# Layer 0 takes x of batches 1 to 7 channel-major from DRAM, with its row statistics turned by a small scratch

## What is computed

```python
# layer 0 (layer 1 differs in the attention)
xn = layernorm(x) * ln_w + ln_b
q = softmax(xn @ Wq + bq, over the 64 channels of a head)
k = softmax(xn @ Wk + bk + mask, over the tokens)
v = (xn @ Wv + bv) * mask
y = q @ (k^T @ v)                       # per head
scale, shift = split(silu(emb) @ W_emb + b_emb)
h = layernorm(y) * (1 + scale) + shift  # ln2_w, ln2_b inside
x = x + silu(h) @ W_out + b_out
```

## Time and profile before

| | before |
|---|---|
| median of 3 runs | 1351.97 us (1345.44 to 1352.27) |
| profiled execution | 1352.28 us, span 1350.5 us |
| TensorE busy | 1311.5 us (97%) |
| VectorE busy | 950.1 us (70%) |
| ScalarE busy | 966.7 us (72%) |
| GpSimd busy | 345.2 us (26%) |
| mean granted clock | 0.967 of full speed |
| chain that ended last | TensorE 75%, ScalarE 12%, VectorE 6%, GpSimd 3%, DMA 1% |

### The profile page before, as it was taken

The page is one execution under the profiler, slowest core; times in us unless marked ns, Lnnn a source line. Parts: engine busy times, 40 slices in busy tenths (PEclk is TensorE's granted clock), DMA queues, the critical chain, the costliest instruction groups (busy, mean ns, idle before and its releaser), DMA issues.

```text
span 1350.5 us, 25321 instructions
## 1 busy us (share of the span) xinstructions
PE 1311.5 (97%) x9592; PEld 1048.4 (78%) x9592; DVE 950.1 (70%) x1930; ACT 966.7 (72%) x2147; POOL 345.2 (26%) x367
## 2 busy tenths in 40 slices
PE   8999999999999999899999999999999999999998
PEld 5788888888888876577787787787787787786666
DVE  5756766666676766666876876876876876877556
ACT  5444344354434548788998998999999999998884
POOL 0323234432334460100500501501501501400302
PEclk9999999999999999899999899899899899899879
DMA  9111111211112356755455455555555545554512
GB/s 336 49 40 63 40 63 62 80 63 40 63 40 87 110 180 190 218 173 158 152 163 158 153 162 158 163 152 158 165 150 158 175 141 157 170 145 126 161 37 87
DMA packets 83994, 173.76 MB, mean 129 GB/s; under 512 B 7304, under 2 KB 8328, under 8 KB 83872
## 3 DMA queue, kind: packets, MB, share of 16 engines
q1 hardware_dynamic: 83872, 172.14, 41.1%
HBM read 104.45 MB, written 67.14 MB: 127 GB/s over the span
## 4 chain that ended last, share of the span: by engine, by line
PE 75%; ACT 12%; DVE 6%; POOL 3%; issue 2%; DMA 1%; SPq 0%; DVEq 0%; POOLq 0%; ACTq 0%
PE ps L526 15%; PE ps L528 14%; PE ps L527 14%; PE ps L705 9%; ACT ps L872 7%; PE ps L521 6%; PE ps L679 6%; PE ps L687 6%; ACT Pb L882 3%; PE ps L630 2%; PE ps L612 2%; POOL yb L1293 1%; DVE st L984 1%; DVE cT L1120 1%; PE ps L540 1%
## 5 line engine op out<-in xcount | busy, mean ns | idle before, releaser
L872 ACT ACTIVATE ps<-ps,cT 128x512 f32<-128x512 f32 x512 | 352.4, 769 | 22.9 <-DVE cT L1120 22.9
L1120 DVE TENSOR_REDUCE cT<-ps 128x1 f32<-128x512 f32 x512 | 321.6, 682 | 66.1 <-PE ps L679 65.8
L882 ACT ACTIVATE Pb<-ps 128x512 f32<-128x512 f32 x512 | 271.3, 669 | 38.4 <-PE ps L687 37.8
L679 PE MATMUL ps<-Ks,Qs 98*128 98x512 f32 x512 | 198.6, 449 | 18.2 <-ACT ps L872 14.7
L679 PEld LDWEIGHTS ps<-Ks,Qs 98*128 98x128 f32 x512 | 100.2, 198 | 80.2 <-ACT ps L872 49.1
L687 PE MATMUL ps<-Qs,Ks 100*128 100x512 f32 x512 | 158.9, 407 | 2.9 <-DVE sg_q L1111 1.2
L872 ACT ACTIVATION_READ_ACCUMULATOR ps<-ps,cT 128x1 f32 x512 | 161.5, 315 | 0.0
L1293 POOL TENSOR_TENSOR yb<-yb,cU 128x512 f32<-128x512 f32 x14 | 20.6, 1486 | 428.0 <-DVE cU L1166 428.0
L687 PEld LDWEIGHTS ps<-Qs,Ks 100*128 100x128 f32 x512 | 95.6, 189 | 38.2 <-ACT Pb L882 11.3
L526 PE MATMUL ps<-xTh,Wh_k 128*128 128x512 f32 x256 | 108.6, 424 | 5.5 <-DVE Wl_k L922 2.9
L1217 POOL TENSOR_TENSOR rs<-ve,mhalf 128x4 f32<-128x4 f32 x32 | 33.0, 1031 | 286.3 <-DVE ve L969 222.8
(11 more groups left out here) (159 smaller groups left out, 2718.0 us busy)
## 6 DMA issues: line engine op xcount, KB each, us to landing
Qs<-stack_scratch SPq DMA_DIRECT2D x32, 768.0 KB
Ks<-stack_scratch SPq DMA_DIRECT2D x32, 768.0 KB
stack_scratch<-sg_q SPq DMA_DIRECT2D x32, 512.0 KB, 2.7
stack_scratch<-sg_k SPq DMA_DIRECT2D x32, 512.0 KB, 2.6
wr<-in_x SPq DMA_DIRECT2D x32, 256.0 KB, 5.0
x_scratch<-wr SPq DMA_DIRECT2D x32, 256.0 KB, 2.0
stack_scratch<-sg_q SPq DMA_DIRECT2D x32, 256.0 KB, 2.9
stack_scratch<-sg_k SPq DMA_DIRECT2D x32, 256.0 KB, 2.9
```

Source lines behind the costliest of these rows:

```text
L679: e.matmul(bank[:], Qs[par][0:RX, j, t * 128:(t + 1) * 128], Ks[par][0:RX, j, :], start=True, stop=True).then_inc(s["S"], 1)
L872: e.activation(bank[:], bank[:], ACT.Exp, bias=nx[:, n % 2, j, t, 0:1], accum_out=dn[:, b % 2, t, 4 * g + j:4 * g + j + 1]).then_inc(s["S_ ...
L882: e.activation(Pb[m][:, j, :], ps[bank_of["a", n, m, j]][:], ACT.Exp).then_inc(s["P"], 1)
L1120: e.tensor_reduce(nx[:, n % 2, j, t, 0:1], ps[bank_of["S", n, j, t]][:], AX.X, ALU.max, negate=True).then_inc(s["S_max"], 1)
```

## The change

For x of batches 1 to 7 (`turned_on_host`) a second DRAM input `xT0` holds x channel-major. Its tile `xr` (1 MB) is loaded beside the token-major `xin`, which is now read by bn_stats only. The two columns per token tile (1/sqrt and -mean/sqrt) are written by GpSimd into `lnc`, turned by four 32 x 32 transposes of VectorE, stored by SP to a DRAM scratch of 2 x 512 values and read back as rows on all 128 partitions (`rn`). A new part `xn`, in the q stage, multiplies and adds these rows on GpSimd, two full-tile operations for each of 4 tiles. Part `tx` has no TensorE work for these batches: VectorE scales and shifts `xr` with ln_w and ln_b, ScalarE copies it to `xTh`, and VectorE writes `xTl` as the difference of two SBUF tiles. The load of the next x waits for the statistics and, with that of the next `xr`, stands behind the last `xTl`. The positions of layer 0's stages and of the seam are other numbers.

```diff
-    "0k": ((0.063, 0.764), (0.503, 1.092)),
-    "0v": ((0.889, 1.145), (0.111, 0.562)),
-    "0q": ((0.659, 1.176), (0, 0.263), (1.065, 1.134)),
-    "0o": ((1.083, 1.166), (0.409, 1.001), (0.43, 0.514)),
+    "0n": ((0.297, 0.652),),
+    "0k": ((0.107, 0.69), (0.373, 0.41)),
+    "0v": ((0.566, 0.962), (0.081, 0.694)),
+    "0q": ((0.486, 0.575), (0.077, 0.696), (1.149, 1.191)),
+    "0o": ((0.67, 0.724), (0, 0.57), (0.041, 0.346)),
...
               ([("mb", 0, 1)] if first else [], 0.1, 0.75),
+              ([] if last else [("xn", b + 1)], *PLAN["0n"][0]),
...
+def turned_on_host(x):
+    return 0 < x < 8
...
+    if k == "tx" and turned_on_host(p[1]):
+        return [], []
...  TensorE
             def tx(i, x, c):
-                if i == 0:
+                if i == 0 and not turned_on_host(x):
...  ScalarE, tx
+                    if turned_on_host(x):
+                        e.wait_ge(s["x_f"], 4 * (x - 1) + c + 1)
+                        e.copy(xTh[:, c, :], xr[:, c, :]).then_inc(s["xT_hi"], 1)
+                        return
...  VectorE, nx
+                if i == 5 and turned_on_host(x):
+                    e.wait_ge(s["x_nr"], x + 1)
+                    if x > 1:
+                        e.wait_ge(s["l_ln0"], 16 * (x - 1))
+                    for u in range(4):
+                        r = e.transpose(lnT[:, 32 * u:32 * u + 32], lnc[32 * u:32 * u + 32, :])
+                    r.then_inc(s["x_T"], 1)
...  VectorE, tx
+                if i == 0 and turned_on_host(x):
+                    p = cols[0]
+                    e.wait_ge(s["xn"], 4 * x + c + 1)
+                    e.tensor_scalar(xr[:, c, :], xr[:, c, :], p[:, c:c + 1], p[:, 4 + c:5 + c],
+                                    ALU.mult, ALU.add).then_inc(s["x_f"], 1)
+                if i == 1 and turned_on_host(x):
+                    e.wait_ge(s["xT_hi"], 4 * x + c + 1)
+                    e.tensor_tensor(xTl[:, c, :], xr[:, c, :], xTh[:, c, :].bitcast(F32), ALU.subtract).then_inc(s["xT_lo"], 1)
+                    return
...  GpSimd
+                    e.tensor_tensor(lnc[:, 0:4], ve[:, 0, :], mhalf[:], ALU.pow).then_inc(s["x_rs"], 1)
...
+                    e.tensor_tensor(lnc[:, 4:8], nm[:, 0, :], lnc[:, 0:4], ALU.mult).then_inc(s["x_nr"], 1)
...
+            def xn(i, x):
+                if i == 0:
+                    e.wait_ge(s["l_ln1"], 16 * x)
+                    e.wait_ge(s["l_xT"], 16 * x)
+                e.tensor_tensor(xr[:, i, :], xr[:, i, :], rn[:, 0, :], ALU.mult).then_inc(s["x_m"], 1)
+                e.wait_ge(s["x_m"], 4 * (x - 1) + i + 1)
+                e.tensor_tensor(xr[:, i, :], xr[:, i, :], rn[:, 1, :], ALU.add).then_inc(s["xn"], 1)
...  SP, tx
-                    e.wait_ge(s["tx"], 4 * x + 4)
+                    if x == 0:
+                        e.wait_ge(s["tx"], 4)
+                    else:
+                        e.wait_ge(s["x_st"], 4 * x + 4)
+                        e.wait_ge(s["xT_lo"], 4 * x + 4)
                     load_x(x + 1)
+                    e.dma_start(xr[:], A["xT0"][x + 1]).then_inc(s["l_xT"], 16)
+
+            def nx_(i, x):
+                if i == 6 and turned_on_host(x):
+                    e.wait_ge(s["x_T"], x)
+                    e.dma_start(lnd.rearrange("a (t n) -> (a t) n", t=NT), lnT[0:8, :]).then_inc(s["l_ln0"], 16)
+                    e.wait_ge(s["l_ln0"], 16 * x)
+                    if x > 1:
+                        e.wait_ge(s["xn"], 4 * x)
+                    e.dma_start(rn[:], lnd.partition_broadcast(128)).then_inc(s["l_ln1"], 16)
```

More of the change, by code:

```diff
@@ L297, in cond_two_layers @@
         qkd = nc.dram_tensor("stack_scratch", [2, 2, 4, RM, T], F32, kind="Internal").ap()
+        lnd = nc.dram_tensor("ln_scratch", [2, T], F32, kind="Internal").ap()
         x1d = nc.dram_tensor("x1_scratch", [B, T, D], F32, kind="Internal").ap()
@@ L355, in cond_two_layers @@
         mB = sb("mB0", [128, T], c=c0)
-        sb("over_sg", [128, NC, D], c=c0)
+        xr = sb("xr", [128, NC, T], c=c0)
         sp = [sb(f"sp{i}", [128, D], c=c0) for i in range(3)]
@@ L369, in cond_two_layers @@
         qrc = sb("qrc", [128, 2, H0], c=c0)
+        rn = sb("rn", [128, 2, T], c=c0)
+        lnc = sb("lnc", [128, 32], c=c0)
+        lnT = sb("lnT", [32, 128], c=c0)
         c0.close()
@@ L406, in l_x, with tx_count @@
             return (s["l_x1"], n) if x % 2 else (s["l_x0"], 16 * 7 + n)
+        def tx_count(x, c):
+            return c + 1 if x == 0 else 4 * (x - 7) + c + 1
         def e_mod(L, h):
@@ L794, in v @@
                         if t == 0:
-                            e.wait_ge(s["tx"], 4 * x + 4)
+                            e.wait_ge(s["tx"], tx_count(x, 3))
                         if x == 8 and t == 0:
@@ L895, in prologue @@
                 e.memset(A0[:], 0.0).then_inc(s["a_set"], 1)
+                e.memset(lnc[:], 0.0).then_inc(s["ln_set"], 1)
                 e.memset(nxs[:].bitcast(F32), 0.0).then_inc(s["nx_set"], 1)
@@ L965, in nx_ @@
                 if i == 4:
-                    if x:
+                    if x == 1 or x > 8:
                         e.wait_ge(s["xn"], 4 * x)
+                    elif x:
+                        e.wait_ge(s["x_nr"], x)
                     e.wait_ge(s["x_mv"], 4 * x + 4)
@@ L1222, in nx_ @@
             def nx_(i, x):
+                if i == 4 and turned_on_host(x):
+                    e.wait_ge(s["x_ve"], x + 1)
+                    if x > 1:
+                        e.wait_ge(s["x_T"], x - 1)
+                    else:
+                        e.wait_ge(s["ln_set"], 1)
+                    e.tensor_tensor(lnc[:, 0:4], ve[:, 0, :], mhalf[:], ALU.pow).then_inc(s["x_rs"], 1)
+                    e.wait_ge(s["x_nm"], x + 1)
+                    e.wait_ge(s["x_rs"], x + 1)
+                    e.tensor_tensor(lnc[:, 4:8], nm[:, 0, :], lnc[:, 0:4], ALU.mult).then_inc(s["x_nr"], 1)
+                    return
                 if i == 4:
                     scales("x", 0, x)
-                if i > 4 and x:
+                if i > 4 and x >= 8:
                     t = i - 5
@@ L1296, in _ @@
             prologue()
-            parts = {"nx": nx_, "ny": ny, "q": q, "qn": qn, "o": o, "ty": ty, "ones": ones, "tlx": tlx}
+            parts = {"nx": nx_, "xn": xn, "ny": ny, "q": q, "qn": qn, "o": o, "ty": ty, "ones": ones, "tlx": tlx}
             for p, i in order:
@@ L1381, in tx @@
                 if i == 1 and c == 3 and x < 7:
-                    e.wait_ge(s["tx"], 4 * x + 4)
-                    load_x(x + 1)
+                    if x == 0:
+                        e.wait_ge(s["tx"], 4)
+                    else:
+                        e.wait_ge(s["x_st"], 4 * x + 4)
+                        e.wait_ge(s["xT_lo"], 4 * x + 4)
+                    load_x(x + 1)
+                    e.dma_start(xr[:], A["xT0"][x + 1]).then_inc(s["l_xT"], 16)
[4 more added lines that the diff above has]
+                    e.wait_ge(s["l_ln0"], 16 * x)
+                    if x > 1:
+                        e.wait_ge(s["xn"], 4 * x)
+                    e.dma_start(rn[:], lnd.partition_broadcast(128)).then_inc(s["l_ln1"], 16)
             def k(i, b, g):
@@ L1414, in ahead @@
                     e.wait_ge(s[f"st{t}"], 16)
-                e.wait_ge(s["tx"], 32)
+                e.wait_ge(s["x_st"], 32)
                 load_x(8)
@@ L1483, in _ @@
             prologue()
-            parts = {"w": w, "m": m, "tx": tx, "k": k, "ty": ty, "o": o, "ahead": ahead, "stacks": stacks, "narrow": narrow, "qk": qk,
+            parts = {"w": w, "m": m, "nx": nx_, "tx": tx, "k": k, "ty": ty, "o": o, "ahead": ahead, "stacks": stacks, "narrow": narrow, "qk": qk,
                      "stack": stack, "nxt": nxt, "lx": lx, "lr": lr, "end": end}
@@ L1514 @@
         "cols1": np.concatenate([col(g[P1 + n]) for n in ("norm_w", "norm_b", "sb_norm_w", "sb_norm_b", "q_b", "k_b", "emb_b")], axis=1),
+        "xT0": np.ascontiguousarray(g["x"].transpose(0, 2, 1).reshape(B, NC, 128, T).transpose(0, 2, 1, 3)),
         "Wq0": g[P0 + "Wq"], "bq0": g[P0 + "bq"], "Wk0": g[P0 + "Wk"],
```

6 lines of the change are left out of this document (3 added, 3 removed), and 4 rows, old and new, of tables (COST, PLAN).

## The result

| | before | after |
|---|---|---|
| median of the runs | 1351.97 us | 1362.61 us (1358.99 to 1363.81) |
| ratio of the medians | | 1.0083 [1.0061, 1.0105] |
| profiled execution | 1352.28, span 1350.5 | 1362.31, span 1360.5 |

The prediction was 1372 in a range of 1345 to 1386, with 0.66 on slower. The side came out, and so did what holds TensorE up; the size is 10.0 us between the two profiled spans, where the sum said 19.8.

A forecast was written before the change was run, and what follows sets the result against it. TensorE's queue was taken to bound layer 0. Middle batches +11.1, batch 0 to 1 +10.0, seam +0.2 and -1.5 make +19.8 us on 1352.28: 1372; own range 1360 to 1384, 1345 to 1386 including the covered case.

The forecast's parts named there:

- undisturbed the chain fits by about 1 us: Middle batches: without turns, last xTl ready at 28.2 us after q's first product, k wanting its fourth at 29.6.
- the scratch and the burst of statistics: Middle batches, k stage: statistics burst and DRAM round trip cost nothing; the burst's ends 0 and 1 us a batch.
- the value of the transposes: Middle batches: TensorE's 16 transposes of x go, 1.75 us a batch, 10.5 us over batches 2 to 7.
- the clock in the middle batches: Layer 0's middle batches: the forecast's sum has no term for a lowered TensorE clock there.
- The stall: k's third and fourth steps wait for xTl, 3.6 us a batch (0 to 4.5), net +1.85 with the transposes gone.
- The replay: o stage with VectorE and GpSimd taking strict turns: subtractions end at 23.5, 26.2, 29.6, 33.1 us after q's first product.
- The third rival: Waits at k's third and fourth steps also lower the clock in each batch, 6 to 10 us more: 1380, chance 0.18.
- Batch 0 to 1: No o stage covers the chain there: k's fourth step +8.3 us, clock +1.7, together +10.0, ends 4 and 12.
- The lower end of 4: Batch 0 to 1: least loss, 4 us, if the statistics row is back from DRAM at once.
- The seam and layer 1: Seam to layer 1: new order -1.5 us (ends -4 and +3), two more changes between products and small blocks +0.2.
- The cover holds: Rival: turns cost the middle batches nothing, 6 x -1.75, batch 1 costs 5.9 plus 1.7 clock: 1348, chance 0.21.
- Faster: Rival: cover holds, scratch returns early and clock stays up, batch 1 costs about 2, seam gives 3: 1341, chance 0.13.

The follow-up runs named there:

- experiment 1: Kernel after, but ScalarE writes xTh and the full value into PSUM and VectorE only subtracts: 1342.16 us, 0.9943 of the kernel before.
- experiment 2: Kernel after without GpSimd's bias sums of o in layer 0 but for one column (result wrong): 1346.73 us, 0.9981 of the kernel before.
- experiment 5: Kernel after without turning and storing the statistics, other DRAM rows loaded instead (statistics wrong): 1359.39 us, 1.0070 of the kernel before.
- experiment 6: Kernel after, but batch 1 prepared the old way with TensorE's transposes: 1351.81 us, 1.0015 of the kernel before.
- experiment 4: Kernel after with GpSimd's second pass over x, the sum, cut to one column: 1348.76 us, 1.0003 of the kernel before.
- experiment 3: Kernel after, but ScalarE writes xTh and the full value back to xr in SBUF, VectorE only subtracts: 1342.50 us, 0.9951 of the kernel before.
- experiment 8: Kernel after with the full value in PSUM for batches 2 to 7 and batch 1 the old way: 1336.52 us, 0.9906 of the kernel before.
- experiment 7: Kernel before with only the changed kernel's positions in layer 0's stages and the seam: 1348.97 us, 0.9991 of the kernel before.

## Why the prediction was right, and where its sizes were off

**What was right.** The cause in the middle batches is the one replayed from the earlier trace rows: VectorE and GpSimd take turns when both work between SBUF tiles. Experiments 1 and 2 show it from both sides, by taking away VectorE's part and half of GpSimd's part of the pairing; experiment 2 alone, with VectorE's work untouched, gives 1.6 of the 2.24 us back. The Trainium skill's page "SBUF — State Buffer", section "SBUF: two separate sides", states the lock. The trace agrees: a subtraction lasts 0.64 us alone and 0.99 to 1.40 beside GpSimd in the timeline above, and in experiment 1 its mean with one operand in PSUM is 0.68. That undisturbed the chain fits by about 1 us was not run as such: experiment 1 fits, but has the scaling on ScalarE. GpSimd's first subtraction came 5.9 us after q's first product (5.8 forecast) and its fourth ended at 20.4 (20.5). That the scratch and the burst of statistics cost the middle batches nothing was right (experiment 5), and so was the value of the transposes: 1.80 us at equal positions and 1.68 against the kernel before, for a forecast of 1.75.

**Luck.** The forecast put the clock in the middle batches at nothing, and it gave 3.2 us of the 10.0. Without these the difference would be 6.8 us, a third of the forecast. On the other side the tail of the profiled execution came out 3.4 us short through the clock, as said below. The two happen to cancel.

**The stall: 2.24 us instead of 3.6.** The replay had k's third step 0.8 and its fourth a further 2.8 us late. The trace has 0 and 2.12 (138.18 against 135.28 + 0.78, the distance of undisturbed steps), with 0.1 for the restart. The step that failed is the length of the turns in the replay, one after another. After q's first product, the four subtractions end at:

| tile | replay | trace |
|---|---|---|
| 0 | 23.5 | 23.2 |
| 1 | 26.2 | 25.8 |
| 2 | 29.6 | 28.7 |
| 3 | 33.1 | 31.8 |

The replay charged VectorE most of a GpSimd instruction each time. In the timelines above GpSimd's is mostly well under way when VectorE asks: the third scaling starts at 132.06 beside a normalisation that runs since 131.67, and the second subtraction (131.50) finds GpSimd waiting for VectorE's reciprocal and lasts 0.64. That saves 0.3 us on the first tiles and 1.3 by the last. The replay also had k ask for its fourth tile at 29.6, where the trace has 29.75, which takes off the rest. The bounds, 0 to 4.5, held it. The net is +0.57 us a batch instead of +1.85.

**The clock in the middle batches: +3.2 us, which the forecast had at nothing.** The third rival said that a rest of some 2 us brings the clock down, each time. It does so in two of the six batches (and in two of six again in experiments 5 and 6, which have the same wait); in none of the six of experiment 4, whose waits are 1.1 to 1.5 us. There the period is 60.2 instead of 58.6, and behind the wait that ends at 196.75 the clock stands low:

```profile
196.00:200.00 4.00, 3.25 (x13) 2.77 (x14) 3.93 (x9) 0.95 (x2) 1.85 (x2) 0.73 0.32 108
200.00:204.00 4.00, 4.00 (x26) 3.67 (x25) 1.35 (x3) 1.50 (x3) 0.00 (x0) 0.84 1.06 396
```

(1 - 0.73) x 4 + (1 - 0.84) x 4 = 1.7 us, the 1.6 of the period. The four other batches rest for the same 1.95 us and keep 1.00. Without a wait (experiments 1, 3 and 8) no period is longer than 56.35. Why two and not six isn't settled. The middle batches thus lost 6 x 0.57 + 2 x 1.6 = 6.6 us: 3.4 by a smaller stall than forecast, less the transposes, and as much again through the clock.

**Batch 0 to 1: +8.3 instead of +10.0.** The links are those of the forecast, and the sizes are these. The power came at 47.48 (46.71 was assumed) and the store was issued at 49.74; it landed within 1.2 us, where 2.0 was taken from the earlier trace rows. GpSimd had the rows at 54.48, where 56.0 was forecast. The broadcast of 512 KB took 3.6 us, less than the 4.5 of the mask's 256 KB. Its source is 4 KB; whether that is why was not tried. From there it took 16.3 us to k's first step (16.5 forecast) and 6.95 to its fourth (7.3). The last tile took no turn, because GpSimd has no bias sums at this boundary: a scaling of 0.54 and a subtraction of 0.69 us. The clock cost 2.0 (1.7 forecast). The planner's numbers, which the prediction had at nothing here, gave 1.07 back (experiment 7). The lower end of 4, for a row that is back at once, was too low: in experiment 5 GpSimd doesn't wait for the row at all, and the loss is 5.2 (55.91 - 50.72).

**The seam and layer 1: -4.9 instead of -1.3.** By its share this is the term that was most off, and it lies outside its lower end of -4. It falls into three stretches:

| | before | after |
|---|---|---|
| q of batch 7 to q of layer 1 | 78.5 | 77.9 |
| from there to the first power of layer 1 | 118.05 | 114.4 |
| from there to the end | 707.8 | 707.1 |

Most of it is the granted clock of these two executions. Summed over windows from q of batch 7 to the end, TensorE stands at 1.2 GHz for 82 us before and for 75 in after. Half of such time is lost, if TensorE is wanted throughout: 41.0 and 37.6 us by this estimate, 3.4 of the 4.9 (1.7 of it in the second stretch). That much comes and goes without any change: in 25 runs of the kernel before the mean clock of the whole goes from 0.966 to 0.972, which is 8 us, and the time from 1345.57 to 1353.42. Without the lost time the tail is 863.4 us before and 861.9 in after: 1.5 less, where the forecast had 1.3. The other seven kernels with channel-major x give 858.2 to 862.1, and the numbers alone, with the transposes still there, 859.8 (experiment 7). So nothing here shows that channel-major x shortens the tail; whether the new positions do by the few us that remain is read from one execution of each kernel, and stays open.

Besides the clock, TensorE's idle time in the second stretch falls from 6.8 to 5.0 us: a wait of 1.5 us for ScalarE's `Pb` is gone, and that for the load of `in_We` fell from 1.0 to 0.2. In the first stretch one of 1.2 us for a load of `Qs` has come, and the wait for `yb`, the only one that I had looked at the earlier trace rows, went from 1.4 to 1.0. The -1.5 of the forecast rested on that wait, so that it agrees with the 1.5 is luck.

**The rivals.** "The cover holds" is refuted for this kernel (TensorE does wait) and describes experiments 1 and 3. "Faster" had the boundary at +2 and fell with it: +8.3. The third was right in two batches of six, and its time, 1380, was not reached.

## What to carry to other kernels

A pass that moves from PSUM to SBUF operands on VectorE is costed not at its own duration but at up to one GpSimd instruction more, wherever GpSimd works from SBUF to SBUF beside it. Here it was 0.35 to 1.0 us more, beside instructions of GpSimd that last 1.05 to 1.6; to charge the whole of one each time overstated the stall. Only what then runs over the end of its cover counts. One such instruction a tile instead of two, or none with one operand kept in PSUM, was worth 2.24 us a batch here. A chain that a steady state hides must be costed again where the steady state begins: the same change lost 8.3 us once between batches 0 and 1, and leaving that batch in the old way gave all of it back. Count the clock with a rest of TensorE, as a chance: a rest of 2 us cost another 1.6 in two of six cases, in each of three kernels. And before a difference of a few us between two profiles is given to the change, compare the time that TensorE's clock was low in both: behind q of batch 7 it was 3.4 us of 4.9.

## What the runs showed of the hardware that I had not expected

**Small VectorE instructions pay the same turn.** Between batches 0 and 1 VectorE forms the scales of layer 0's conditioning, on 8 columns. Before, GpSimd had one subtraction there (54.60, 1.04 us) and was idle from 55.64 on:

```profile
54.51 0.62 DVE L944 TENSOR_SCALAR mod<-ps,cols 128x8 f32<-128x8 f32 x4
55.17 0.92 DVE L949 SCALAR_TENSOR_TENSOR mod<-mod,cols 128x8 f32<-128x8 f32 x4
56.12 0.63 DVE L953 TENSOR_SCALAR mod<-mod,cols 128x8 f32<-128x8 f32 x4
```

Beside GpSimd's passes over x they took:

```profile
54.42 0.63 DVE L966 TENSOR_SCALAR mod<-ps,cols 128x8 f32<-128x8 f32 x4
55.09 3.34 DVE L971 SCALAR_TENSOR_TENSOR mod<-mod,cols 128x8 f32<-128x8 f32 x4
58.46 3.69 DVE L975 TENSOR_SCALAR mod<-mod,cols 128x8 f32<-128x8 f32 x4
```

The last two lines take seven microseconds for 1.6, 0.6 to 0.8 more for each instruction. A scaling of 512 columns pays 0.76 to 1.0 more in the timeline above: the price hangs on the number of instructions far more than on their width. The first line, which reads PSUM, pays nothing, though GpSimd's first product starts at 54.48 beside it. The loss hid behind GpSimd's chain here.

**One instruction, several prices.** The same 128x512 scaling from SBUF to SBUF lasted 0.50 us alone and 1.26 to 1.50 beside GpSimd; the same bias sum on GpSimd 1.30 us with VectorE reading PSUM and 1.60 with VectorE in SBUF. VectorE's scaling rises by a factor of 2.5 to 3 and its subtraction by 1.5 to 2.2, GpSimd's instructions by a little over a fifth.
